# Identity products on TensorE during its early waits, and weight, gate, row and bias work of the first two batches placed elsewhere

## The reference, cut to what matters

```python
x = ln(x + L0(x));  x = ln(x + L1(x));  x = ln(x + L2(x));  x = ln(x + L3(x))
# L0: y = (adj @ x + x) @ w0 + b0;  y / max(norm(y), 1e-12)
# L1: A = exp(8 tanh((x q)(x k)^T / sqrt(128) / 8)) * adj;  A / rowsum(A) @ x @ v
# L2: (si + sj^T + adj * w_r + g_b) @ x @ w2 + b2
# L3: relu of a Chebyshev sum over adj (three weights w3) + b3
```

## Time and profile before

| | us |
|---|---|
| median of 3 runs | 725.24 |
| lowest and highest | 724.34, 726.21 |
| the profiled execution, its own time | 723.83 |
| its span in the profile | 721.6 |
| PE busy, share of the span | 641.3, 89% |
| DVE busy, share | 588.1, 81% |
| ACT busy, share | 407.5, 56% |

### The profile page before, as it was taken

One profiled execution on the slowest core, in us unless ns is written; L12 is line 12 of the kernel. 1 busy time (PEld: TensorE's weight loads), 2 busy tenths in 40 slices (PEclk: granted clock), 3 DMA queues, 4 the chain that ended last, 5 costly groups with the idle time before them and its releaser, 6 DMA issues. The chain is left out here.

```text
span 721.6 us, 17445 instructions
## 1 busy us (share of the span) xinstructions
PE 641.3 (89%) x7398; PEld 475.4 (66%) x7398; DVE 588.1 (81%) x1521; ACT 407.5 (56%) x711; POOL 74.0 (10%) x49
## 2 busy tenths in 40 slices
PE   5597577899999899999999899999999899869894
PEld 2354444558866796658866796658866796538794
DVE  5859988678998898978998898978998897879535
ACT  6369569324592657736592658636592558523512
POOL 0111110002001110012001110012001110021002
PEclk9899888999999999999999999999999999989998
DMA  9510000001000110002000100001000100000102
GB/s 338 196 68 0 1 1 1 1 1 31 2 2 1 28 35 1 2 1 60 2 2 2 34 29 1 1 2 59 2 2 2 31 2 1 2 0 3 31 3 59
DMA packets 12446, 18.75 MB, mean 26 GB/s; under 512 B 592, under 2 KB 9040, under 8 KB 12368
## 3 DMA queue, kind: packets, MB, share of 16 engines
q1 hardware_dynamic: 12368, 17.63, 7.3%
HBM read 13.44 MB, written 4.19 MB: 24 GB/s over the span
## 5 line engine op out<-in xcount | busy, mean ns | idle before, releaser
L238 POOL TENSOR_TENSOR small<-small,minus_half 128x8 f32<-128x8 f32 x39 | 69.6, 1788 | 625.8 <-DVE small L562 322.2
L382 ACT ACTIVATE att<-r,coef 128x1024 f32<-128x1024 f32 x64 | 70.2, 1098 | 51.3 <-PE r L1208 51.3
L834 DVE TENSOR_TENSOR att<-att,adjT 128x1024 f32<-128x1024 f32 x64 | 78.1, 1220 | 16.2 <-ACT att L384 16.1
L1206 PE MATMUL r<-xq,a_hi 128*128 128x128 f16 x448 | 75.5, 219 | 3.8 <-DVE xq L785 3.8
L839 DVE SCALAR_TENSOR_TENSOR p_lo<-p_hi,att 128x1024 f16<-128x1024 f16 x64 | 77.9, 1219 | 0.0
L1206 PE MATMUL r<-rs,a_hi 128*128 128x128 f16 x448 | 75.8, 219 | 0.4
L1208 PE MATMUL r<-rs,a_lo 128*128 128x128 f16 x448 | 75.8, 219 | 0.0
L1207 PE MATMUL r<-rs,a_hi 128*128 128x128 f16 x448 | 75.8, 219 | 0.0
L1208 PE MATMUL r<-xq,a_lo 128*128 128x128 f16 x448 | 75.4, 219 | 0.0
L1207 PE MATMUL r<-xq,a_hi 128*128 128x128 f16 x448 | 75.4, 219 | 0.0
L384 ACT ACTIVATE att<-att,coef 128x1024 f32<-128x1024 f32 x64 | 73.5, 1149 | 2.1
(11 more groups left out here) (380 smaller groups left out, 2085.7 us busy)
## 6 DMA issues: line engine op xcount, KB each, us to landing
adjT<-in_adj_t SPq DMA_DIRECT2D x8, 512.0 KB, 8.1
x<-in_x SPq DMA_DIRECT2D x7, 512.0 KB, 4.8
out<-outb SPq DMA_DIRECT2D x7, 512.0 KB, 3.5
pq<-in_adj SPq DMA_DIRECT2D x2, 512.0 KB, 8.3
u<-in_adj SPq DMA_DIRECT2D x2, 512.0 KB, 9.0
tmp<-in_adj SPq DMA_DIRECT2D x2, 512.0 KB, 9.7
x2s<-in_adj SPq DMA_DIRECT2D x2, 512.0 KB, 10.3
outb<-in_x SPq DMA_DIRECT2D x1, 512.0 KB, 11.3
```

The source lines that it names most:

```text
L238: return nc.gpsimd.tensor_tensor(dst, src, minus_half[:], ALU.pow)
L382: nc.scalar.activation(att[:, s], dst[:], ACT.Tanh, scale=c_tanh).then_inc(S["th"], 1)
L834: tt(att[:, s], att[:, s], adjT[:, t, :], ALU.mult).then_inc(S["pm"], 1)
L1206: mm(dst, s_hi, m_hi, start=start, stop=False, skip_group_check=True)
```

## The change

It does six things.

- PE: `keep_busy(n)` issues n matmuls of 512 columns, the scaled identity times a block of ones, into `r0`, which nobody reads. It is called with 9 ahead of the first maximum's sum, with 2 behind it, with 11 ahead of the first chunk of `adj @ x`, and with 15 ahead of `adj @ x` of batch 1.
- PE: the sum of the first weights' maxima moves up from the fifth to the fourth chunk. In the attention of batch 0 the layer-0 projection of batch 1 and the second sum of maxima go ahead of the second chunk of scores. The sum for batch 2's input maximum goes into the attention of batch 1.
- ACT: `adjT` is multiplied in place by 2048 * 16 (`scale_adj`, eight copies), and the exponential has no bias any more.
- ACT: `degrees` and `v_scaled` are ordered anew; `bias_rows` moves from the attention of batch 1 to `back(1)`.
- DVE: the third layer's weights and the later maxima go ahead of the attention of batch 0, as do the two additions of b0 for batch 1 (`y_half`); the second scales go behind the first `mask`.
- DVE: the input maximum of batch 2 goes into the attention of batch 1, behind the statistics of `ln_begin(1, 0)`; the splits of the later weights (`weights_split(3, 4)`) go behind its fifth low part.

```diff
+            def scale_adj(first, last_):
+                for c in range(first, last_):
+                    act.wait_ge(S["adj_lo"], c + 1 if c < C - 1 else C + 1)
+                    copy(adjT[:, c], adjT[:, c], LO_UP * P_UP).then_inc(S["adj_up"], 1)
...
-                nc.scalar.activation(att[:, s], att[:, s], ACT.Exp, scale=TANH_CAP, bias=c_exp).then_inc(S["ex"], 1)
+                nc.scalar.activation(att[:, s], att[:, s], ACT.Exp, scale=TANH_CAP).then_inc(S["ex"], 1)
...
+                scale_adj(0, 3)
                 y0_hi(0, 0, r1[:, half(0)])
                 y0_hi(0, 1, r1[:, half(1)])
+                degrees(0, 3)
                 x0_hi(1)
-                degrees(0, 4)
+                scale_adj(3, C)
+                degrees(3, 4)
...
-                degrees(7, 8)
                 y0_hi(1, 1, av[:, 2])
                 v_hi(0, r1)
-                v_scaled(0)
-                act.wait_ge(S["const_ok"], 1)
                 for t in range(C):
                     exponent(0, t)
+                    if t == 0:
+                        v_scaled(0)
+                        degrees(7, 8)
...
                 x0_lo(1)
+                third_layer_weights()
                 rows.residual()
                 ln_begin(0, 0, xas[0])
                 weights_split(1, 2)
-                y0_lo(1, 0, m7[:])
+                later_max()
                 ln_shift(0, 0)
                 ln_norm(0, 0, xas[0])
+                y0_lo(1, 0, m7[:])
...
+                rows.y_half(0, r2)
+                rows.y_half(1, r2)
+                dve.wait_ge(S["adj_up"], C)
                 mask(0, 0)
+                weights_scale(1, slice(3, 5))
+                second_coefs()
...
                 ln_begin(1, 0, xas[0])
+                x0_max(2)
                 mask(1, 1)
...
                 p_lo_part(1, 4)
+                weights_split(3, 4)
+                w_ch.end()
...
+            def keep_busy(n):
+                for _ in range(n):
+                    mm(r0[:, half(0)], ident_up[:], x1T[:, 0, half(0)], start=True, stop=True)
...
             for c in range(C):
-                if c == 4:
+                if c == 3:
                     weights_sum(0, 0, 3)
...
                 layer0_half(0, 1, r1)
+                keep_busy(15)
                 pe.wait_ge(S["x_lo"], 2)
...
                 scores(0, 0)
+                layer0_half(1, 0, r2)
+                layer0_half(1, 1, r2)
+                weights_sum(1, 3, 5)
                 pe.wait_ge(S["v_lo"], 2)
                 scores(0, 1)
-                layer0_half(1, 0, r2)
-                layer0_half(1, 1, r2)
```

More of the change, by code:

```diff
@@ L104, in adj_resnorm @@
         coef = sb("coef", [P, 8])
-        c_w0, c_tanh, c_v, c_l2, c_u, c_o, c_exp = (coef[:, j:j + 1] for j in range(7))
+        c_w0, c_tanh, c_v, c_l2, c_u, c_o = (coef[:, j:j + 1] for j in range(6))
         deg, dis, dis2, root_deg, eps_deg, r_scale, q_scale = (sb(n_, [P, C]) for n_ in ("deg", "dis", "dis2", "root_deg", "eps_deg", "r_scale", "q_scale"))
@@ L159, in adj_resnorm @@
         names = ("w_in bc_in wq_in iu_ok x_in x1_in ident_ok const_ok m_cp w3_c m_mm w_max w_sum w_red w_ok wj_c "
-                 "adj_hi adj_lo deg_ok sc_ok b3_ok "
+                 "adj_hi adj_lo adj_up deg_ok sc_ok b3_ok "
                  "norm_sq norm_r dis_ok x_max x_sum x_st x_hi x_lo "
@@ L434, in start @@
                         copy_x2(0)
-                    if t == 4:
-                        bias_rows()
                 p_hi_part(1, C - 1)
@@ L452, in back @@
                 last = i >= 2
+                if not last:
+                    bias_rows()
                 act.wait_ge(S["y0_mm"], 2 * (i + 1))
@@ L588, in _ @@
             nc.vector.memset(one_sj[:, :, 0:1], 1.0)
-            nc.vector.memset(c_exp, float(np.log(LO_UP * P_UP)))
+            nc.vector.memset(x1T[:, 0, half(0)], 1.0)
             nc.vector.memset(vhis[0][:, :, D:D + 1], 1.0)
@@ L635, in first_max, with third_layer_weights @@
                 weights_max(0, (w0_sb, m_sb, v_sb))
-            def second_max():
+            def third_layer_weights():
                 ch = Count(dve, S["w3_c"], 0, 2)
@@ L644, in second_max, with later_max @@
                 ch.end()
+            def later_max():
                 weights_max(3, (w2_sb[:], w3c.rearrange("p k d -> p (k d)")))
@@ L933, in start @@
                     if t == 1:
-                        rows.y_half(0, r2)
-                        rows.y_half(1, r2)
-                    if t == 2:
                         rows.stats_half(0)
@@ L939, in start @@
                         rows.arg()
+                    if t == 2:
+                        row_scales()
                     if t == 3:
-                        row_scales()
-                        second_max()
+                        rows.residual()
                     if t == 4:
-                        rows.residual()
+                        ln_begin(0, 1, xas[1])
                     if t == 5:
-                        ln_begin(0, 1, xas[1])
-                    if t == 6:
                         ln_shift(0, 1)
                         ln_norm(0, 1, xas[1])
-                        weights_scale(1, slice(3, 5))
-                        second_coefs()
+                    if t == 6:
                         gate_weights()
@@ L954, in start @@
                 x1t_lo(1, r0)
-                weights_split(3, 4)
-                w_ch.end()
-                x0_max(2)
                 g_lo(1, r1)
@@ L963, in start @@
                 l_.then_inc(S["e1a"], 1)
-                x0_scale_read(2)
                 mask(1, 0)
@@ L976, in start @@
                 p_lo_part(1, 2)
+                x0_scale_read(2)
                 x0_scales(2)
@@ L1193, in _ @@
             mm = nc.tensor.matmul
+            def keep_busy(n):
+                for _ in range(n):
+                    mm(r0[:, half(0)], ident_up[:], x1T[:, 0, half(0)], start=True, stop=True)
+            pe.wait_ge(S["const_ok"], 1)
+            pe.wait_ge(S["iu_ok"], 1)
+            keep_busy(9)
             pe.wait_ge(S["x_max"], 1)
-            pe.wait_ge(S["const_ok"], 1)
             mm(m7[:, 4:5], ones[:], xmax[:], start=True, stop=True).then_inc(S["x_sum"], 1)
+            keep_busy(2)
             pe.wait_ge(S["wq_in"], 16)
@@ L1202, in _ @@
             pe.wait_ge(S["ident_ok"], 3)
+            keep_busy(11)
             def split_product(dst, s_hi, s_lo, m_hi, m_lo, start, stop):
@@ L1277, in _ @@
             pe.wait_ge(S["x_lo"], 1)
-            pe.wait_ge(S["iu_ok"], 1)
             for c in range(C):
-                if c == 4:
+                if c == 3:
                     weights_sum(0, 0, 3)
@@ L1370, in start @@
                     next_scores(0, t)
-                    if t == C - 1:
-                        weights_sum(1, 3, 5)
                     attend(0, t - 3)
@@ L1380, in start @@
                 attend(0, 7)
-                row_max_sum(2)
                 v_product(1, r0)
@@ L1391, in start @@
                 next_scores(1, 4)
+                row_max_sum(2)
                 attend(1, 1)
```

## The result

The changed kernel takes 714.59 us (median of 4 executions, 714.53 to 716.16) beside 724.79 for the kernel before on the same chip: a ratio of 0.9866, interval 0.9839 to 0.9893. It is faster, as forecast. Measured twice more, on other chips, the same kernel gave 716.47 and 717.95. All its 14 executions have their median at 716.5 (714.49 to 719.68), the 42 of the kernel before at 724.6 (722.62 to 726.47). The gain over all of them is 8.1, where the sum of the forecast had 8.2. That agreement is luck: a gain that was put too low and losses that were not foreseen make up for each other.

The account below looks back on a forecast made before the run. Bound: PE at half clock, DVE waiting on slow PE, and DVE pacing both attentions in batches 0 and 1. -6.5 and -1.7 gave -8.2 from 723.83, 715.6; the median, 1.4 above, gave 717.0, range 715.2 to 720.8 (8 in 10).

Parts of the forecast that it names:

- The first wait: DVE's 2.72 us wait for the sum of the first weights' maxima, in the first chunks, would go: -2.7 us.
- The copies: ACT's eight in-place copies of adjT, 1.0 us each, would cost nothing, with 1.3, 1.5 and 2.3 us of cover.
- the layer norm: Batch 1, behind adj @ x: first transposes at 39.3 instead of 43.67, second four -4.9, first tanh -5.2 us.
- the moved work of batch 0: Batch 0's attention: DVE stays the bound and 4.1 us of work leave its path: -7.3 at the last low part.
- Rivals 3 and 4: 3: DVE's moved work shows more, 720 to 723, chance 0.08; 4: in-place ACT copies make the kernel slower, chance 0.03.
- Rival 1: Clock stays low at the start, batch 1's adj @ x or g products: 718.1 to 721.1, chance 0.25.
- the step on that place: Batch 1's adj @ x: full clock behind a 2.0 us gap, so the 4.9 us half-clock stretch becomes 2.4.
- The step on the `g` products: Batch 1's g products: full clock behind a wait of about 1.4 us, shift from -7.5 to -8.6 us.
- The give-backs: Batch 1's attention: +0.7 us for batch 2's input maximum, +1.3 us for the later weights' splits, both no longer hidden.
- The exponential: On ACT, each exponential without its bias column is 0.1 us shorter: -1.7 us over all batches.
- the one on the later batches: Batches 2 to 6: the shorter exponential removes PE's 0.20 us wait for one attend a batch, -1.0 us in all.
- Rival 2: The exponential on ACT stays at 1149 ns without its bias: 718.7 us, chance 0.1.

## Why the prediction was right, and where not

**Direction and mechanism.** The first wait is gone for -2.8 (forecast -2.7), and batches 0 and 1 together are 5.4 or 6.8 us shorter, depending on the execution. The run of products alone (-3.4), of the exponential alone (-1.4), and of the moves with the exponential but no products (-5.3) show that the products and the exponential each carry a share. The moved work was not run alone: its share is what those two leave.

**The copies, the layer norm, the moved work of batch 0.** In the execution with full clock the first transposes stand at 39.28, the first tanh at 46.93, the second mask at 53.23 and the end of the last low part at 81.44; the forecast had 39.3, 47.0, 53.5 and 81.7. Rivals 3 and 4 fall by these numbers and by copies of 0.97 us.

**Rival 1, the clock.** I gave 0.25 to one or two places at half clock, as if the kernel had one answer. It has several: with a gap of 2.0 us before it, batch 1's `adj @ x` ran at full clock in one execution and partly at half in another, 1.5 us apart. Of the eight traces with that gap, four have full clock and four have half. In the step on that place, "I take full clock" should have read "in some executions". The step on the `g` products was right in all three profiles of the changed kernel, though the wait ahead of them was 0.48 us and not 1.4.

**The give-backs.** 0.7 and 1.3 in the forecast; 0.71 and 1.28 by the two runs that undo one each, 1.97 together.

**The exponential** is the term that was mis-sized, and with it the range. The forecast took 0.1 for the instruction (measured 0.091) and -1.7 for the term: 0.3 in batches 0 and 1, 1.0 in batches 2 to 6, 0.4 in the last. Measured is -2.65: 0.33, 1.87 and 0.45. So the step that failed is the one on the later batches, where the forecast had -0.2 each, "the wait of 0.20". It is -0.37 each. Besides the wait that the earlier trace rows shows, PE loses 0.16 us between the last scores and the first attend of a batch, too short for the timeline to mark as a wait: 0.37 us apart with the column (0.38 in the run of products alone, 0.37 in the run with a column of zeros), 0.21 without it. I had read one wait where there were two. The Trainium skill, "ScalarE: Activation LUTs", section "What ACT_TABLE_LOAD costs", has 93 ns for a per-partition pointer; the run with a column of zeros agrees with 91. Rival 2, an exponential that stays at 1149 ns, falls with it.

**The sum and the range.** For an execution with full clock the sum should have been -6.5 - 2.65 = -9.15 instead of -8.2; measured were -9.3. The forecast then added 1.4 us, since the median of three executions lay that much above the profiled one. Over 42 executions that distance is 0.7, so half of it was chance. The forecast of 717.0 is 2.4 above the first measurement, and these two terms are 0.95 and 1.4 of it: three of those four executions lie near 714.6, beside the 714.49 of the one that was profiled with full clock. (That these three had full clock too is likely and not shown, as they have no trace.) The range ended at 715.2, since below the forecast it left room only "for an exponential that gains more". The trace of before is one execution; the range had no room for how executions of one kernel differ.

Over all 14 executions the forecast is only 0.5 too high. There the losses of clock that it had not counted, some 1.2 us by difference, cover most of the 0.95 and of the 0.7. That is the luck named at the start.

**What stays open.** Four places gain or lose from one execution to the next: the start (1.5 us), 30 to 34 us (1.5), 130 to 137 us (1.7), and the last batch behind PE's wait of 5.45 us (83.36 to 84.63 us from there to the end in the fourteen traces, the later ends mostly with the longer half clock). An estimate from these: full clock in the first three and the shortest end give 713.7, all four losses 719.7, and the executions of the changed kernel lie from 714.49 to 719.68. The loss at the start goes with a later `x` in the one trace shown, but `x` was taken up at 4.92 in the run with 24 products, behind which PE waited 0.86 us, and there the clock was up before 6.2. For the other places no wait or instruction compared ahead of them differs by more than a few hundredths, and no run here tells what decides. At 30 us the gap reads 2.01 in the four traces with half clock and 2.02 in the four with full clock. That hundredth is the last digit of the timeline, and whether it is a cause, a sign of one or chance is not shown. Nor is it shown that the three medians of the changed kernel (714.59, 716.47, 717.95) differ for these reasons alone, as only one execution of each has a trace.

## What to carry to other kernels

Where a clock that comes and goes decides, take more than one execution before a single profile's stretch is made a term, and give the range one such stretch on either side. Filler ahead of a load should be no longer than the wait at the slower clock: eleven products that hid at 2.54 us held the work up by 1.3 us at 3.70. A gap between two instructions can hide a wait that no timeline marks, so compare the distance of the same two instructions in both kernels before a wait is priced. Work that "fills idle time" has to be costed at its new place too: two helpers moved ahead of their need cost 2.0 us by the traces. The kernel with both put back measured 713.14, ratio 0.9839 with an interval of 0.9817 to 0.9862, below those of the changed kernel (0.9866 to 0.9899 in three measurements), though it overlaps the interval of the first.

## What the runs showed of the hardware

- The granted clock of TensorE differs between executions of one and the same program: behind a gap of 2.01 us one execution of the changed kernel had half clock for some 3.4 us, behind 2.02 us another had full clock. With the gap at 5.25, in the kernel before, in the run of the exponential alone and in the two runs without the fifteen products, the profile had half clock each time. From 130 to 137 us, behind the same waits, seven of eleven profiles of the changed kernel and its variants had it. In the last batch, behind a wait of 5.45 us, all fourteen traces have a stretch of half clock, and from there to the end it is 83.36 to 84.63 us.
- Half clock need not cost anything: from 98 to 107 us the mean granted clock was 0.57 in one execution of the changed kernel and 0.81 in another, and from the scores ahead of it to batch 1's `yT` it was 34.10 us in both.
- A column as the bias of an exponential over 128x1024 float32 costs 91 ns on ScalarE (1149 against 1058), even when it holds zeros.
- At the start the page grants 1.00, while nine products take 0.44 us each and the next eleven 0.23: there the durations tell the clock, and the granted value does not.
